# Relative attention over eight batch groups on one core: the fourth group's values halved around two outputs, the weight turns drawn ahead of two other VectorE steps, GpSimd's clears behind a rounding, and one of its subtractions in four pieces

## The reference

```python
h = (x - mu) * jax.lax.rsqrt(var + 1e-05) * gamma + beta
q = (h @ Wq).reshape(I, B, H, F)
k = (h @ Wq).reshape(I, B, H, F)
v = (h @ Wv).reshape(I, B, H, F)
content = jnp.einsum('ibnf,jbnf->ijbn', q + u_bias, k)
pos = _left_shift(jnp.einsum('ibnf,jnf->ijbn', q + v_bias, r))
attn = jax.nn.softmax((content + pos) / sqrt_d, axis=1)
o = jnp.einsum('ijbn,jbnf->ibnf', attn, v).reshape(I, B, H * F)
return o @ Wout + bout
```

## Time and profile before

| | |
|---|---|
| median of 3 runs | 833.94 us (831.2 to 836.29) |
| time of the profiled execution | 833.91 us |
| its span | 832.1 us |
| outside the span | 1.8 us |
| TensorE busy | 793.4 us, 95% of the span |
| VectorE, ScalarE, GpSimd busy | 521.0, 311.5 and 301.2 us |
| granted TensorE clock, mean | 0.993 of full speed |
| relative attention, first `group_scores` of the loop to the first `out_product` | 318.19 to 372.34 us |

### The profile page before, as it was taken

The page is one execution under the profiler, slowest core; times in us unless marked ns, Lnnn a source line. Parts: engine busy times, 40 slices in busy tenths (PEclk is TensorE's granted clock), DMA queues, the critical chain, the costliest instruction groups (busy, mean ns, idle before and its releaser), DMA issues.

```text
span 832.1 us, 16698 instructions
## 1 busy us (share of the span) xinstructions
PE 793.4 (95%) x6401; PEld 582.3 (70%) x6415; DVE 521.0 (63%) x1175; ACT 311.5 (37%) x827; POOL 301.2 (36%) x154
## 2 busy tenths in 40 slices
PE   4899999999999998989999999899999999999996
PEld 4555455545557777877877777688888888888883
DVE  5779777987754436576788888864473443343334
ACT  4312332333253428752257665723413111211211
POOL 0000000000162933543022221343639999994033
PEclk9999999999999999999999999999999999999999
DMA  9968555865502022021169100040476554541147
GB/s 348 378 229 315 199 210 229 317 227 204 215 21 83 1 60 96 2 87 48 52 232 384 44 0 0 2 152 1 163 259 215 172 202 151 175 152 50 53 117 259
DMA packets 46572, 127.00 MB, mean 153 GB/s; under 512 B 4000, under 2 KB 8352, under 8 KB 40368
## 3 DMA queue, kind: packets, MB, share of 16 engines
q1 hardware_dynamic: 36752, 105.44, 34.9%
q10 hardware_dynamic: 7200, 12.32, 4.2%
q0 software_dynamic: 2560, 8.39, 3.1%
HBM read 101.99 MB, written 24.15 MB: 152 GB/s over the span
## 4 chain that ended last, share of the span: by engine, by line
PE 78%; DVE 8%; ACT 3%; DMA 3%; issue 3%; POOL 2%; SPq 0%; another core or an unknown queue 0%; DVEq 0%; ACTq 0%; POOLq 0%
PE scores L592 11%; PE bank L625 11%; PE bank L1126 7%; PE bank L1128 7%; PE bank L1127 6%; ACT sp L1613 2%; PE bank L805 2%; PE bank L682 2%; PE bank L840 2%; POOL picked L1366 2%; PE bank L684 2%; PE bank L683 2%; PE bank L559 2%; PE bank L870 2%; PE bank L928 2%
## 5 line engine op out<-in xcount | busy, mean ns | idle before, releaser
L1812 DVE STREAM_TRANSPOSE ctxT<-nat 128x1024 f32<-128x1024 f32 (+3 forms) x124 | 116.8, 1005 | 2.2 <-DMA nat<-in_ctx_keys 2.0
L625 PE MATMUL bank<-nat,probT 128*64 128x512 f32 (+1 forms) x416 | 96.0, 606 | 0.1
L592 PE MATMUL scores<-ctxT,hn 32*64 32x385 f32 (+5 forms) x2048 | 88.4, 487 | 2.6 <-DVE ctxT L1812 1.3
L1233 POOL TENSOR_TENSOR wq_lo<-wq_raw,wq_hi 128x1024 fp32r<-128x1024 f32 x4 | 9.5, 2405 | 223.4 <-ACT wq_hi L1457 223.4
L1353 POOL TENSOR_TENSOR ring_lo<-ring_raw,ring_hi 128x2048 fp32r<-128x2048 f32 x18 | 83.0, 4612 | 15.1 <-ACT ring_hi L1700 14.0
L592 PEld LDWEIGHTS scores<-ctxT,hn 32*64 32x64 f32 x2048 | 62.0, 131 | 25.9 <-issue 16.4
L1126 PE MATMUL bank<-ring_hi,xg_lo 128*128 x180 | 74.2, 412 | 0.4 <-DVE xg_lo L2432 0.4
L1128 PE MATMUL bank<-ring_hi,xg_hi 128*128 x180 | 70.6, 392 | 0.0
L1127 PE MATMUL bank<-ring_lo,xg_hi 128*128 x180 | 70.1, 390 | 0.0
L625 PEld LDWEIGHTS bank<-nat,probT 128*64 128x64 f32 (+1 forms) x416 | 29.5, 138 | 53.8 <-issue 52.5
L2444 DVE TENSOR_TENSOR rhm_lo<-bank,rhm_hi 128x512 fp32r<-128x512 f32 x21 | 14.5, 692 | 79.5 <-ACT rhm_hi L1711 75.9
(11 more groups left out here) (310 smaller groups left out, 1879.8 us busy)
## 6 DMA issues: line engine op xcount, KB each, us to landing
nat<-in_ctx_keys SPq DMA_DIRECT2D x48, 1024.0 KB, 7.3
ring_raw<-in_Wexp SPq DMA_DIRECT2D x21, 1024.0 KB, 6.3
x_slots<-zeros SPq DMA_DIRECT2D x1, 5632.0 KB, 17.7
y_slots<-zeros SPq DMA_DIRECT2D x1, 5632.0 KB, 32.4
hn<-x_slots ACTq DMA_DIRECT2D x22, 256.0 KB, 4.3
y_slots<-hn ACTq DMA_DIRECT2D x22, 256.0 KB
w_raw<-in_Wexp SPq DMA_DIRECT2D x3, 1024.0 KB, 5.7
nat<-in_ctx_keys SPq DMA_DIRECT2D x16, 130.0 KB
```

The lines of the kernel that those rows point to most:

```text
L592: last = nc.tensor.matmul(scores4[64 * b:64 * b + 64, i, 0:keys_in[i]], q4[rows_i, j, 64 * b:64 * b + 64], ctxT[rows_i, b, j, 0:keys_in[i] ...
L625: last = nc.tensor.matmul(bank[7][64 * b:64 * b + 64, :], probT[0:n, j, 64 * b:64 * b + 64], nat[k % 2][0:n, b, j, :], start=j == 0, stop= ...
L1812: dve.transpose(dst, src).then_inc(columns_ready, 1)
```

## The change

Four edits, none of which adds or removes arithmetic:

1. `group_values(3)` stood whole between `group_output(0)` and `group_scores(3)`. Its first half now stands ahead of `group_output(0)` and its second half between `group_scores(3)` and `group_output(1)`. ScalarE's list follows: `group_exps(2)` ahead of `group_out(0)`, then the first half's copy, `group_high(4)`, the second half's copy, and `group_exps(3)` ahead of `group_out(1)`.
2. On VectorE `group_turned(g + 1)` moves from behind `group_low(g + 3)` and `group_out(g)` to right behind `group_inv(g + 1)`, in all six turns.
3. GpSimd's clears wait for `ohi_ready` 2 in place of `o_full` 16.
4. `w_lo[2]` is subtracted in four instructions of 512 elements a partition in place of one of 2048.

```diff
-            def group_values(g, par):
+            def group_values(g, par, halves=range(2)):
                 pe.wait_ge(hg_act, g + 1)
                 pe.wait_ge(hg_dve, g + 1)
-                for h in range(2):
+                for h in halves:
                     pe.wait_ge(v_out, 2 * g + h - 1)
                     value_products(par, h, range(HC))
...
-            for g in range(NG - 2):
+            for g in range(2):
+                group_scores(g + 2, g)
+                group_values(3, 1, (g,))
+                group_output(g, g)
+            for g in range(2, NG - 2):
                 group_scores(g + 2, g % 2)
                 group_output(g, g % 2)
-                if g != 1:
-                    later = 3 if g == 0 else g + 2
-                    group_values(later, later % 2)
+                group_values(g + 2, g % 2)
...
-            pool.wait_ge(o_full, 2 * NG)
+            pool.wait_ge(ohi_ready, 2)
...
-            nc.gpsimd.tensor_tensor(w_lo[2][:], w_raw[2][:], w_hi[2].bitcast(F32)[:], ALU.subtract).then_inc(wlo_ready, 1)
+            for c in range(HC):
+                last = nc.gpsimd.tensor_tensor(w_lo[2][:, c, :], w_raw[2][:, c, :], w_hi[2].bitcast(F32)[:, c, :], ALU.subtract)
+            last.then_inc(wlo_ready, 1)
...
             group_exps(1, 1)
+            group_exps(2, 0)
             group_out(0)
-            group_exps(2, 0)
-            values_out(3, 1)
-            for g in range(1, NG - 2):
+            act.wait_ge(o_full, 2)
+            values_out(3, 1, (0,))
+            group_high(4, 0)
+            values_out(3, 1, (1,))
+            group_exps(3, 1)
+            group_out(1)
+            for g in range(2, NG - 2):
...
+            group_turned(0, 0)
             for g in range(NG - 2):
-                group_turned(g, g % 2)
                 group_max(g + 2, g % 2)
                 group_inv(g + 1, 1 - g % 2)
+                group_turned(g + 1, 1 - g % 2)
                 if 1 <= g < NG - 3:
                     dve.wait_ge(v_full, 2 * g + 4)
                     group_low(g + 3, (g + 3) % 2)
                 group_out(g)
-            group_turned(NG - 2, 0)
             group_inv(NG - 1, 1)
             group_turned(NG - 1, 1)
```

More of the change, by code:

```diff
@@ L1554, in _ @@
                 group_exps(g + 2, g % 2)
-                if g >= 2:
-                    weight_high(wout_hi, wout_raw, w_loaded["wout"], WOUT_PIECES[g])
-                    values_out(g + 2, g % 2)
+                weight_high(wout_hi, wout_raw, w_loaded["wout"], WOUT_PIECES[g])
+                values_out(g + 2, g % 2)
             group_out(NG - 2)
```

## The result

The changed kernel took 826.12 us (median of 4 runs, 825.11 to 827.49), the kernel before 833.72 beside it: ratio 0.9894, 95% interval 0.9868 to 0.992, faster by 7.6 us by the medians and by 8.8 us by the ratio. One of the 34 runs of before that stand beside the single edits took 2055.79 us and is left out of their ratios. The profiled execution took 827.49 us (span 825.7) against 833.91.

The account below looks back on a forecast made before the run. TensorE, busy 95% of the span, was taken as the bound, so only its gaps could be won: 4.94 us up to the first product plus 0.9 in the third, 833.91 - 5.85 = 828.1 us; range 825.0 to 831.8, leaving out 2 in 10.

Parts of the forecast that it names:

- the sum: Whole kernel: first product 4.94 us earlier plus 0.9 in the third product, 5.85 us off 833.91, giving 828.1.
- the worth of edit 3: Ahead of the first output product: VectorE's rounding no longer meets GpSimd's clears, so the product starts 1.3 us sooner.
- edit 4: Third output product: with the subtraction in four pieces, TensorE's 0.77 us wait and slower restart go, 0.9 us; lower bound 0.
- Edits 1 and 2, up to output 2: TensorE from scores 2 to values of group 4: no waits left, those values start at 331.67, 4.72 us earlier.
- The wait at output 7: TensorE, last group output: a new wait of 1.05 us, starting at about 364.6 instead of 363.5; bounds 0 and 1.4.
- VectorE waiting out one whole GpSimd instruction: VectorE beside GpSimd: stretched casts wait for one GpSimd instruction to end, such as the first clear, 1.85 us.
- The rival of the run of instructions: Low part of group 6: VectorE waits through several GpSimd instructions, first product about 2 us later, 830.0 us; chance 0.09.
- the fall behind output 2: TensorE after the 2.15 us gap there: clock at 1.2 GHz costs about 1.6 us more, counted as recovered.
- the second rival: After the change, the clock falls around output 7 or the first product instead, costing 1.6 us: 829.7 us; chance 0.12.
- its own range: Whole kernel time if the forecast holds: 826.3 to 829.8 us, given a chance of 0.56.

Follow-up runs that it names:

- the variant of the change: Changed kernel with piece 3 of Wout's low part moved on GpSimd from turn 5 to 6: 821.97 us, 0.9878 against before; repeated, 824.17 us, 0.9913.
- the two later comparisons: The unaltered changed kernel timed twice more against the kernel before: 823.73 us, 0.9903 [0.9879, 0.9928], and 825.83 us, 0.991 [0.9876, 0.9944].
- the run with 14 fillers: Kernel before plus 14 overwritten 128x128 matmuls in each TensorE gap, ahead of output 2 and of the first product: 828.95 against 829.48 us, 0.9989.

## What of the prediction was right, and which steps failed

Two terms of the sum failed: the worth of edit 3, that is the price of the gap ahead of the first product, and edit 4. The other terms held.

**Edits 1 and 2, up to output 2: right.** Forecast 4.72 us earlier, values of group 4 at 331.67; 331.42 in the trace. In three traces of the full change output 2 waited 0, 0 and 0.52 us. The runs of one edit alone left 2.15 and 1.36 us.

**The wait at output 7: right.** Forecast 1.05 us at 364.6, measured 1.21 at 364.60, and 1.08 and 0.65 us in the two further traces of the change. Its cause is the one worked out: moving piece 3 by one turn removes the wait and, with it, 1.4 us of the stretch. The details on VectorE were only partly those forecast. The low part of group 7 took 2.21 us as expected, that of group 6 only 0.69; two biases took 1.93 and 2.15 us instead. With piece 3 moved they still took 1.81 and 2.02 us and nothing waited at output 7, so the wait hangs on the low part of group 7.

**Edit 3: direction right, size too small (first failed step).** The first product came at 367.43, as forecast, and the gap ahead of it fell by 1.36 us. But 1.3 us is the worth only where the rounding had waited for one clear and the clock stayed up behind the gap, as in the one execution that the prediction read. Taking the edit out of the change cost 3.1 us by the medians. The step "VectorE waiting out one whole GpSimd instruction" failed in one of four traces of before: it waited for both, 3.49 us, at 1.74 us more. The Trainium skill ("SBUF — State Buffer", Who interferes with whom) says the pair goes to whoever starts first, for the whole instruction. Three traces (1.75, 1.75, 1.76 us) agree, the fourth does not: GpSimd kept it through the next clear as well. The rival of the run of instructions was thus real at another place than the one it was written for.

**Edit 4: wrong (second failed step).** Forecast 0.9 us; leaving the edit out of the change cost 0.04 us of stretch. The prediction held that the low part of o starts when it does in the earlier trace rows, so that only its length counted. The traces show that its start moves. ScalarE rounds the down weights when their load has landed, and its rounding of o, on which the low part waits, stands behind that. The weights' rounding began 5.5, 7.1, 7.3 and 7.8 us after the first product in the four traces of before, and the stage from the first product to the last low pass lost 0, 0.4, 0.7 and 1.2 us. In the change without edit 4 it began 6.7 us after, and nothing was lost. Four pieces may still be worth something when it comes later: at 7.1 us the variant of the change lost nothing where before lost 0.4. At 8.6 us the run with the edits on GpSimd alone lost 0.8 us even so. Why the load lands when it does was not tested. In the first pair of traces this stage did get 1.17 us shorter, close to the 0.9 of the sum. That the sum of 5.85 met the 5.99 of the traces is in this part luck: the time was won, but not by edit 4.

**The clock: the part of edit 3 that was left at nothing.** The prediction took the fall behind output 2 as part of the 4.72 us and the other gap as costing its idle time, because its window showed 1.00 in that one execution. The runs show that either gap can bring the clock down: behind the one at output 2 in four traces of four of before, behind the one ahead of the first product in one of these four and in the traces of edit 1, of edit 2 and of both together. A fall costs 1.6 us: the stage from the first product to the last low pass takes 43.7 to 43.8 us with one, and 42.1 to 42.25 without one where nothing in the third product is late. Filling both gaps gained 2.6 us by the medians, filling the first alone 1.4. Edit 3 therefore is also worth the chance of a second fall. How often it comes is not settled. The mean clock of all runs is 0.9941 and 0.9934 before against 0.9970 and 0.9963 after in the two later comparisons, 0.0029 in each, 2.4 us, where one fall (0.17 of 10 us) is 1.7 us. But the 0.7 us beyond the one fall is no more than the same kernel differed from itself. The mean also counts falls elsewhere: in the profiled executions the clock fell between 220 and 240 us in 16 of 18, between 30 and 50 us in 8. This is the second rival turned round: a rival on where the clock falls was asked of the kernel after and not of the one before.

**The sum.** Forecast 5.85 us; 5.99 between the first two traces, 5.8 between the means of four of before (97.68) and three of after (91.88), which contain both the longer rounding and the second fall once; 6.7 to 7.6 by medians, 7.5 to 8.8 by the ratios. The forecast of 828.1 stood for an execution with one fall and one clear, and was 2 us too slow; the measured 826.12 lies just below its own range. With 3.1 us for edit 3 in place of 1.3 and nothing for edit 4 the sum is 3.63 + 3.1 = 6.7 us (an estimate from the forecast's other terms and the medians). That is the lower end of the medians, but no trace shows it in one execution. About a microsecond or more between the traces and the medians stays open: of the three intervals of the change only the last one reaches down to 5.8. The wait at output 0 is a candidate. It is the load of the position scores that sets it: in eight traces with such a wait and all 24 matmuls in one piece, the wait and the time from VectorE's first use of these scores to the scores of group 2 add up to 6.1 us each. It was 0.7 to 1.6 us in four traces of before and 3.0 in one with filler, and the traces are too few to say what it is on average.

## What to carry to other kernels

A gap of the engine that bounds the kernel can have a price beside its length, and one trace shows one draw of it: look at two or three traces of the same kernel before pricing a gap, and compare a stretch, not the whole time. The same holds for a wait that hangs on when a load lands: an edit that shortens one instruction is worth only what it wins at that moment. Where VectorE has a short cast on the critical path, order GpSimd's long instructions behind it by a semaphore, and also the ones that follow at once. Two reorderings that close one gap can each leave most of it open alone (2.15 and 1.36 us of 2.15 here).

## What the runs showed of the hardware

- Work put into an idle stretch of TensorE can make a kernel faster: 16 matmuls without use, 3.8 us, for 2.6 us less by the medians (0.9974 [0.995, 0.9997]), and 14 of them, 3.4 us, in the first gap alone for 1.4 us less (0.9977 [0.9963, 0.999]).
- Gaps of 2.15 and 2.16 us were followed by a fall in some executions and not in others of the same place; a wait of 3.00 us (output 0 of the run with 14 fillers) was not, and the waits of 1.6 us and below never were, in the stretch that was read. The Trainium skill ("TensorE: Matmul & The Clock Gate", The HAM clock gate) describes the fall as following idle time; the traces agree that every fall in this stretch followed a gap, and with gaps as short as these.
- A VectorE scaling of 128 x 8 elements, 0.17 us by itself, takes 1.93 us beside GpSimd's addition to the queries and 2.15 us beside its subtractions: the number of elements does not protect an instruction.
- A VectorE cast of 128 x 256 elements took 0.29 us with no GpSimd clear running, 1.75 us when it came just behind the start of one, and once 3.49 us, through two clears.
- A matmul of 128x128 in full float32 takes about 0.24 us and leaves two records in the trace: eight are x16 and 2.02 us, 14 are x28 and 3.36 us.
